# Dense deformable sampling: y offsets copied to all 32 channel partitions by DMA instead of spread by TensorE

## The reference, cut to what matters

```python
offsets = conv2d(x, offset_w, offset_b)          # 18 channels: 9 dy, 9 dx
mod = sigmoid(conv2d(x, mod_w, mod_b))           # 9 channels
sy = base_y + offsets[:, :9]; sx = base_x + offsets[:, 9:]
y0, x0 = floor(sy), floor(sx); wy1, wx1 = sy - y0, sx - x0
sampled = (1-wy1)*((1-wx1)*g00 + wx1*g01) + wy1*((1-wx1)*g10 + wx1*g11)
out = einsum('bckp,ock->bop', sampled, weight) * mod.mean(axis=1) + bias   # k: 9 taps
```

## Time and profile before

| | |
|---|---|
| median of three runs | 3088.52 us |
| profiled execution | 3089.17 us |
| its span | 3087.0 us |
| dense sampling of group 0, first to last instruction | 1239.08 to 1783.7 us |
| dense sampling of group 1 | 2536.25 to 3087.0 us |
| PE busy over the span | 2441.5 us (79%) |
| DVE, ACT, POOL busy | 1802.2, 1536.3, 1010.3 us |

### The profile page before, as it was taken

The page is one execution under the profiler, slowest core; times in us unless marked ns, Lnnn a source line. Parts: engine busy times, 40 slices in busy tenths (PEclk is TensorE's granted clock), DMA queues, the critical chain, the costliest instruction groups (busy, mean ns, idle before and its releaser), DMA issues. The chain is left out here.

```text
span 3087.0 us, 98767 instructions
## 1 busy us (share of the span) xinstructions
PE 2441.5 (79%) x44813; PEld 1566.7 (51%) x44813; DVE 1802.2 (58%) x2813; ACT 1536.3 (50%) x1757; POOL 1010.3 (33%) x740
## 2 busy tenths in 40 slices
PE   0775992749999639699999916699994578999998
PEld 0673341537777415255555505477773344555555
DVE  5894656235555454477777661455554545777774
ACT  1222444225555434366667632355553435666765
POOL 0331001035555200444444210455551014444441
PEclk7897996869999859699999958799997687999999
DMA  1567615011110352122222250101115321222221
GB/s 44 160 205 135 97 28 218 4 41 27 37 27 27 137 215 64 52 84 85 85 84 79 72 223 21 31 27 30 30 30 209 149 54 65 84 85 85 80 82 61
DMA packets 244300, 258.54 MB, mean 84 GB/s; under 512 B 79596, under 2 KB 174368, under 8 KB 243872
## 3 DMA queue, kind: packets, MB, share of 16 engines
q1 hardware_dynamic: 234656, 218.58, 24.3%
q0 software_dynamic: 9216, 33.56, 2.7%
HBM read 153.52 MB, written 98.57 MB: 82 GB/s over the span
## 5 line engine op out<-in xcount | busy, mean ns | idle before, releaser
L2146 PE MATMUL dense_spread<-dense_cp,kept_spread_yx 32*128 32x512 f32 x2432 | 479.2, 665 | 67.5 <-DVE dense_cp L2305 60.3
L1433 ACT ACTIVATE snake_samp<-snake_s 128x1024 f32<-128x1024 f32 x320 | 321.1, 1023 | 299.7 <-PE snake_s L1363 299.5
L2325 DVE TENSOR_TENSOR dense_hat<-dense_spread,dense_hat 128x1024 f32<-128x1024 f32 x256 | 301.5, 1219 | 250.2 <-PE dense_spread L2146 250.2
L1496 DVE TENSOR_SCALAR snake_hat<-snake_spread 128x1024 f32<-128x1024 f32 x256 | 301.4, 1219 | 205.6 <-PE snake_spread L1341 205.6
L2250 ACT ACTIVATE dense_hat<-dense_spread 128x1024 f32<-128x1024 f32 x256 | 248.7, 1022 | 283.7 <-PE dense_spread L2146 277.5
L1363 PE MATMUL snake_s<-snake_hat,snake_xt 64*64 64x128 f32 x10240 | 337.5, 274 | 19.4 <-ACT snake_samp L1433 19.1
L2196 PEld LDWEIGHTS dense_s<-dense_hat,dense_xt 64*64 64x64 f32 x11264 | 267.8, 134 | 145.3 <-issue 95.5
L2270 ACT ACTIVATE dense_samp<-dense_s 128x864 f32<-128x864 f32 (+1 forms) x384 | 299.2, 833 | 78.5 <-PE dense_s L2196 78.4
L1363 PEld LDWEIGHTS snake_s<-snake_hat,snake_xt 64*64 64x64 f32 x10240 | 284.9, 134 | 86.0 <-issue 42.2
L2196 PE MATMUL dense_s<-dense_hat,dense_xt 64*64 64x108 f32 x11264 | 308.9, 257 | 0.5
L667 PE MATMUL dcnoff_acc<-xn,kept_w_off 32*32 32x512 f32 x4608 | 176.6, 620 | 153.0 <-PEq L46 153.0
(11 more groups left out here) (319 smaller groups left out, 3731.2 us busy)
## 6 DMA issues: line engine op xcount, KB each, us to landing
dense_cp<-offs SPq DMA_DIRECT2D x576, 56.0 KB
x<-blur_x SPq DMA_DIRECT2D x16, 1024.0 KB, 5.0
pre<-snake_ob SPq DMA_DIRECT2D x32, 512.0 KB, 4.0
dense_xr<-x SPq DMA_DIRECT2D x64, 256.0 KB, 3.2
out<-dense_xr SPq DMA_DIRECT2D x64, 256.0 KB, 2.5
gateconv_low<-x SPq DMA_DIRECT2D x24, 512.0 KB, 9.5
dense_cp<-offs SPq DMA_DIRECT2D x256, 48.0 KB
offs<-dcnoff_cm SPq DMA_DIRECT2D x64, 144.0 KB
```

Source lines behind the costliest of these rows:

```text
L1433: act.activation(samp[u % 2][:, :, i * MS:(i + 1) * MS, :, :].rearrange("p b m t h -> p b (m t h)"), sample_at(u, i)[:, :, :], ACT.Copy).t ...
L1496: ins = dve.tensor_scalar(strided(hat[u % 2][:, 0:1], GUARD + (4 * tau + 2 * half) * SW * SR, [[8, 2], [SW * SR, 2], [SR, SW], [1, 8]]), s ...
L2146: return pe.matmul(bank[:, :], k.spread_yx[r, kind, :], cp[u % 2][r, tile, :], start=True, stop=True)
L2325: dve.tensor_tensor(h, p_hat[pair][:, :, :].rearrange("p t (r x) -> p (t r) x", x=W), h, ALU.mult).then_inc(main_ready, 1)
```

## The change

The y factor no longer passes through TensorE. SP copies the y offsets of a band from DRAM straight to all 32 partitions of each image, for taps 0 to 3 (`ys[0]`, 8 KB in a partition) and taps 4 to 8 (`ys[1]`, 10 KB), with four DMAs each, one for an image. ScalarE computes relu(y + 1 - r) from them into `hat`, with a bias per partition (`y_shift`). The clamp at 1 is done in the product: VectorE computes min(hat, 1) times the spread x factor in one scalar_tensor_tensor. TensorE spreads x only. For this `offs` is stored in another order (bands outermost, then image, band of four rows, channel), so that the taps of one image and band are contiguous. `ys` and `xr` have one buffer each; before, `xr` had two. Patches' guard columns are dropped from `samp`, `mod` and `hat`, so that `weigh` reads 256 columns instead of 264 in a matmul. `w_dcn` keeps only its diagonal blocks of 64x64.

```diff
-        hat = [s.sb(f"hat{i}", [P, K2, 4, PC]) for i in range(2)]
-        xr = [s.sb(f"xr{i}", [P, 4, W]) for i in range(2)]
+        ys = [s.sb(f"ys{i}", [P, len(p), BX]) for i, p in enumerate(PARTS)]
+        hat = [s.sb(f"hat{i}", [P, K2 * BX + 2 * PW]) for i in range(2)]
+        xr = s.sb("xr", [P, 4, W])
...
+            def load_x(u):
                 for i in range(4):
+                    at = offs[u // 4, 0, u % 4, K2 + 2 * i, 0, 0:1]
+                    sp.dma_start(cp[u % 2][32 * i:32 * i + 32, 0:2, :],
+                                 bass.AP(tensor=at.tensor, offset=at.offset, ap=[[0, 8], [4 * OFF_CH * BX, GI], [1, 2 * BX]])
                                  ).then_inc(loaded[u % 2], 16)
+                at = offs[u // 4, 0, u % 4, 2 * K2 - 1, 0, 0:1]
+                sp.dma_start(cp[u % 2][0:32, 2, :], bass.AP(tensor=at.tensor, offset=at.offset, ap=[[0, 8], [4 * OFF_CH * BX, GI], [1, BX]])
+                             ).then_inc(loaded[u % 2], 16)
+                sp.dma_start(cp[u % 2][64:64 + GI, 2, :], offs[u // 4, :, u % 4, MOD, :, :].rearrange("b h w -> b (h w)")).then_inc(loaded[u % 2], 16)
+
+            def load_y(u, part):
+                for b in range(GI):
+                    at = offs[u // 4, b, u % 4, PARTS[part][0], 0, 0:1]
+                    sp.dma_start(ys[part][32 * b:32 * b + 32, :, :].rearrange("p t x -> p (t x)"),
+                                 bass.AP(tensor=at.tensor, offset=at.offset, ap=[[0, 32], [1, len(PARTS[part]) * BX]])
+                                 ).then_inc(y_in[part], 16)
...
             for u in range(NB4):
                 if u + 2 < NB4:
+                    for part in range(2):
+                        sp.wait_ge(y_kept[part], u + 2)
+                        load_y(u + 2, part)
                 if u >= 1:
+                    store(u - 1)
+                if u + 3 < NB4:
+                    sp.wait_ge(mod_spread, u + 2)
+                    load_x(u + 3)
+                if u >= 1:
+                    sp.wait_ge(stored, 16 * u)
+                    load_x3(u)
...
         @block.scalar
+            def keep_y(u, part):
+                act.wait_ge(y_in[part], Y_LOADS * (u + 1))
+                if part == 0 and u >= 2:
+                    act.wait_ge(sampled, SG * (u - 1))
+                t0, nt = PARTS[part][0], len(PARTS[part])
+                act.activation(hat[u % 2][:, t0 * BX:(t0 + nt) * BX], ys[part][:, :, :].rearrange("p t x -> p (t x)"), ACT.Relu,
+                               bias=k.y_shift[:, :]).then_inc(y_kept[part], 1)
...
         @block.vector
             def products(u, i):
+                dve.wait_ge(y_kept[i], u + 1)
                 for pair in range(2):
                     dve.wait_ge(x_spread, 4 * u + 2 * i + pair + 1)
-                    dve.tensor_tensor(h, p_hat[pair][:, :, :].rearrange("p t (r x) -> p (t r) x", x=W), h, ALU.mult).then_inc(main_ready, 1)
+                    dve.scalar_tensor_tensor(h, h, 1.0, p_hat[pair][:, :, :].rearrange("p t x -> p (t x)"), ALU.min, ALU.mult
+                                             ).then_inc(main_ready, 1)
```

TensorE's new calls. In `spread_x` the two matmuls of a pair (`at` 0 and 1) now read the same block of 32 partitions:

```diff
+            def spread_x(u, i):
                 for pair in range(2):
+                    if i == 1:
+                        pe.wait_ge(main_ready, 4 * u + pair + 1)
+                    elif pair == 0:
+                        pe.wait_ge(x_clipped, u + 1)
+                        if u > 0:
+                            pe.wait_ge(hat_ready, u)
+                            pe.wait_ge(mod_kept, u)
+                    elif u > 0:
+                        pe.wait_ge(main_ready, 4 * u)
                     for at in range(2):
+                        ins = spread(p_hat[pair][:, at, :], u, 2 * i + pair, at, 0)
                     ins.then_inc(x_spread, 1)
             def spread_last(u):
                 pe.wait_ge(main_ready, 4 * u + 3)
+                spread(p_hat[0][:, 0, :], u, 0, 2, 0).then_inc(last_spread, 1)
+                spread(p_hat[0][:, 1, :], u, 2, 2, 1).then_inc(mod_spread, 1)
```

268 lines of the change are left out of this document (104 added, 164 removed).

## The result

The changed kernel took **3107.6 us** as the median of 12 runs (3094.4 to 3117.6), against 3089.9 for 12 runs of the kernel before (3087.5 to 3093.8): a ratio of 1.0049, 95% interval 1.0036 to 1.0063. It is slower by half a per cent, where I had forecast 3028 us. Its profiled execution took 3101.79 us (span 3099.4).

A forecast was written before the change was run, and what follows sets the result against it. TensorE's list bounds the kernel before (15.71 us a band), the DMA queue the changed one (15.3). Per group -15 + 30 x (15.3 - 15.71) - 1.4 - 1.5 = -30, twice -60: 3028 us; own range 2990 to 3075, 8 in 10 2958 to 3190.

The forecast's parts named there:

- third round of band 0 after the first memset: Start of each group: band 0's third sampling round at +36 us instead of 50.8, 15 us less a group.
- 30 bands: Dense stage between the third rounds of bands 0 and 30: 15.3 us a band instead of 15.71.
- from the third round of band 30 to the group's end: End of each group: last two bands without x loads, last pieces without some spreads, 1.4 + 1.5 us less.
- The call of four spreads: TensorE, x spreads: only two of four matmuls side by side on two row blocks, 2.05 us a call.
- rival 3: TensorE: a held matmul holds all behind it, call 3.4 us, round trip 17.3 us, 3157 us in all; chance 0.06.
- The product: VectorE, hat times spread x: 1.219 us before, 0.06 added for scalar_tensor_tensor, 1.28 us.
- the round trip: Each band's chain over VectorE and TensorE from one second x spread to the next: 14.6 us.
- rival 1: DMA queue keeps up (13.7 us at 251 GB/s), 14.6 us round trip bounds: 2987 us, about 2957 at 14.1; chance 0.28.
- the sum of the DMA queue: Per band in one queue: y loads 11.0 us, x loads 2.9, store and x3 1.4, together 15.3 us.
- the queue stays fed: DMA queue: between two loads of one ys buffer 9 us of other work, more than ScalarE's 2.4 us.
- rival 2: DMA queue slow: y loads at 176 GB/s, 17.7 us a band, 3172 us in all; chance 0.28.
- the chance of slower: Whole kernel: 0.35 for slower, against 0.60 for faster by over 0.2% and 0.05 for within 0.2%.

The follow-up runs named there:

- e2: Changed kernel with y loads fetching only half their elements from band 1 on (a measurement, not a usable version): 2961.4 us, ratio 0.959 to the kernel before.
- e3: Changed kernel with eight one-tap x loads, so that a spread call's four matmuls lie on four row blocks: 3091.4 us, ratio 0.9998 to the kernel before.
- e9: Changed kernel with y rows cut into 2 KB by access pattern; packets stayed 8 and 10 KB, so effectively a second run of it: 3110.0 us, ratio 1.0068.
- e13: Changed kernel with the six x loads of a band issued by GpSimd in its own queue from band 3 on: 3108.2 us, ratio 1.007 to the kernel before.
- e10: Changed kernel with the y loads' outermost source dimension 8 instead of 32, so eight engines carry each load: 3100.6 us, ratio 1.0026 to the kernel before.
- e17: Kernel before, with 2.1 MB a band copied between unused places in HBM by two GpSimd DMAs: 3165.5 us, ratio 1.024.
- e5: Changed kernel with, in group 1 only, a second xr buffer and x3 loaded early, ahead of the store: 3148.7 us, ratio 1.019 to the kernel before.
- e12: Changed kernel with y loads in image order 0, 2, 1, 3 and, in group 1 only, second xr buffer and early x3 load: 3074.6 us, ratio 0.994.
- e16: As e12, but x3 loaded behind the x loads, its place in the changed kernel: 3047.3 us, ratio 0.985 to the kernel before.
- e6: Changed kernel with the four y loads of a part issued for images 0, 2, 1, 3: 3041.1 us, ratio 0.983 to the kernel before.

## Why the prediction was wrong

Made against the profiled execution, 3029 was forecast and 3101.8 measured, 72.8 too little. By its own steps:

| step | forecast us | measured us | missed, two groups |
|---|---|---|---|
| third round of band 0 after the first memset | 36 | 43.5 and 41.9 | +13.4 |
| 30 bands | 15.3 each | 16.08 and 16.57 | +61.5 |
| from the third round of band 30 to the group's end (for group 0: to group 1's first memset) | -2.9 against before | -2.4 and -1.4 | +1.9 |
| before group 0 | 0 | -4.6 | -4.6 |

(The other 0.6 us is rounding.)

**The TensorE side was right.** The call of four spreads on two blocks took 1.99 us for 2.05, on four blocks 1.14, and a weighing 4.12 for 4.11. Held matmuls did not hold the others: rival 3 (3.4 us a call) is out. `keep_y` took 2.00 and 2.43 us for 2.01 and 2.44. The product took 1.217: the 0.06 that I had added to 1.219 was not there. With the two clamps (0.84 and 0.42 for 0.805 and 0.543), the ninth product (0.68 for 0.75) and the spreads these small things make the round trip 14.1 and not 14.6. e2 shows it bare at 14.05, 2961 us, where rival 1's text had 2957 for 14.1.

**The failed step is the sum of the DMA queue, 15.3 us a band.** e3, with the same bytes and 1.7 us less for TensorE to do, has 16.0; so has e9. Of its terms y was right: 2.36 MB at 218 GB/s are 10.8 us (forecast 214 and 11.0). So were the x loads: 0.60 MB at the 209 GB/s of this stretch are 2.9.

```profile
2843.00:2845.00 2.00, 2.00 (x44) 1.44 (x40) 1.07 (x1) 1.29 (x2) 2.00 (x2) 1.00 0.52 209
```

What is left, 16.0 - 10.8 - 2.9 = 2.3 us, is for store, `x3`, the small packets at the ends and the instruction packets; I had 1.4 for it, from the rate of 4 KB rows for transfers of 2 KB rows. The packet times that the expectation of e13 adds up for the busiest engines say the same: y 10.6 us (11.0 forecast), x 3.1 (2.9), store and `x3` 1.8 (1.4), small and instruction packets 0.4, for which I had nothing, together 15.9. e3's share of 0.91 is what a queue leaves that never rests and has 2.9 of 16.0 us on half the engines, (13.1 + 2.9/2)/16.0 = 0.91, so "the queue stays fed" held there. So 0.7 us of the missing 1.0 a band are terms of the sum that were too small, some 40 us in all.

**What the prediction did not have is the half-clock band.** The product of 62 bands and one duration supposed that all are alike. Ten of 60 took 19.9 us. I had written the round trip at the full clock throughout, because the earlier trace rows show 1.00 with TensorE never idle; the change takes away just that.

What these bands cost in the end is not isolated. This profiled execution lies 0.33 us a band above e3's 16.0, and the medians lie 3107.6 - 3091.4 = 16 us apart. Against putting all of that down to the slow bands speaks e9's profiled execution, the same program with ten of them and bands of 16.00 us: the queue runs ahead in a slow band, and the bands behind it go at 14.1 to 14.6. Nor is the half clock a loss by itself: in the 60 intervals e3 has it for 149 of 959 us, the changed kernel for 123 of 976. e3's shorter list fits beside the queue all the same.

What begins such a band I read in the trace and did not show by experiment. There are two beginnings. Six of the ten, all in group 1, stand behind a gap in the middle of a sampling round, 1.4 to 2.8 us long and called issue, which ended 1.3 to 1.5 us behind a packet of 16 KB of the instruction queue. (Two more such gaps, of 1.2 and 1.8 us, have no slow band behind them.) The DMA part of the profile for the gap at 2768.79 (queue, packets, MB, share):

```profile
q1 hardware_dynamic: 89, 0.60, 97.5%
q8 instruction: 1, 0.02, 3.1%
```

One packet of instructions came among 89 of the data queue. e2, with the share at 0.62, has no such gap. The Trainium skill ("Runtime: NRT & Kernel Launch", Instruction fetch mechanics) calls this fetch mostly hidden behind the work; before the change agree, here the six gaps speak against it.

The other four, the three of group 0 among them, stand behind waits of 2.4 to 3.5 us for VectorE's product, and VectorE had itself waited 5.0 to 7.6 us for `x3`, late in the queue. (Like waits elsewhere have 3.4 us at the half clock behind them, too short to reach a weighing.) One of the four on VectorE and TensorE, and the clock behind it:

```profile
1457.62 0.75 DVE L2328 SCALAR_TENSOR_TENSOR dense_xr<-dense_mod,kept_par,dense_xr 128x512 f32<-128x512 f32 x1 [5.84 <-DMA dense_xr<-x]
1459.55 2.08 PE L2164 MATMUL dense_spread<-dense_cp,kept_spread_x 32*128 32x512 f32 x4 [3.19 <-DVE dense_hat L2313]
1459.00:1473.00 14.00, 13.45 (x116) 7.04 (x120) 7.40 (x8) 7.35 (x6) 7.08 (x5) 0.52 0.91 226
```

So in this trace late data alone is enough, and e10, without one gap of the first kind and with seven slow bands, says the same. That late instructions begin the other six stays likely, not shown: e9 and e17 were to settle it and did not.

**The start** waited for the last piece of y. The timeline of group 1 has ScalarE take up the second part of band 1 here:

```profile
2571.69 2.43 ACT L2248 ACTIVATE dense_hat<-dense_ys,kept_y_shift 128x2560 f32<-128x2560 f32 x1 [2.73 <-DMA dense_ys<-offs]
```

That is 38.6 us behind the memset, where my queue order had it landed at 33. In between the engines moved less than the 214 to 227 GB/s I had counted with:

```profile
2541.00:2549.00 8.00, 3.79 (x8) 1.20 (x8) 4.10 (x5) 2.00 (x1) 3.25 (x3) 0.50 1.01 217
2551.00:2559.00 8.00, 5.12 (x11) 1.44 (x7) 3.04 (x3) 4.38 (x3) 3.04 (x3) 0.50 1.07 180
2563.00:2569.00 6.00, 5.58 (x71) 3.36 (x69) 1.64 (x3) 3.37 (x2) 2.71 (x2) 0.57 0.61 131
```

217 GB/s in the first y loads; 180 at a full share where x loads of band 1 on eight engines and y loads run together; 131 at a share of 0.61 behind that. I read it as the upper eight engines, which have no x loads, running ahead of the lower eight. In e10, where y and x loads both use eight engines, the interval from band 0 to band 1 is 16 us instead of 22. That fits and was not tested by itself.

**The ring.** In the chain the ring through `xr` takes most of group 1, and it is the symptom that misled me: e5, e12 and e16 took it away in group 1, and it was slower than group 0 of the same execution by 2.1, 1.3 and 0.8 us a band (0.5 in the changed kernel, 0.0 in e6). Store and `x3` land late because they stand behind 10.8 us of y loads in a queue that never rests; waiting for them less freed nothing. Why the group got slower rather than stayed is open. The rate fell in each (198, 209 and 221 against 225, 231 and 230 GB/s in group 0 of the same run), and most of e12's loss goes with the place of the `x3` load (3074.6 us with it early, 3047.3 in its old place).

**What the right sum would have given.** With 16.0 in it the text's arithmetic is -15 + 30 x (16.0 - 15.71) - 2.9 = -9 a group, 3071 for the execution: still faster by 0.6%, at an effect far below the 2% that I named. The rest up to 3101.8 is the start (+13), the 0.33 us a band by which this execution lies above 16.0 (+20, read as slow bands and not shown), and little else; in e9's profiled execution, with 16.00, the same program took 3090.4, no more than before. That the kernel is slower rests on the medians of 12 and 5 runs, 3107.6 and 3110.0. The forecast and rival 2 were one mechanism, the queue above the round trip; the y rate was the forecast's, and the chance of slower, 0.35, was carried by the wrong cause.

## What to carry to other kernels

When a change moves work from an engine with a full list into a DMA queue, add up every transfer of the queue from a row with its own row length, small packets and instruction packets too, and treat a result within half a microsecond of the old band as no gain. A queue that is nearly full has costs that no sum shows: data, and it seems instructions too, arrive late, TensorE stands still for 1.4 to 3.5 us and then runs at half the clock for 7 to 14 us. Whether that costs time depends on what slack its list has. Before adding buffers or queues, look at which partitions follow each other: loads into 32 partitions that alternate between 0 to 63 and 64 to 127 gave 2% for a change of one line, and freeing the buffer that the chain showed gained nothing. Before calling a second queue useless, look whether its transfers ran beside those of the first.
